# First attention: reciprocals of the sums in the loop, spread by a ones product; keys over twelve steps and weighing in each next step

## What is computed

```python
q = (query @ Wq).reshape(b, sq, NUM_HEADS, HEAD_DIM).transpose(0, 2, 1, 3)   # query = layernorm(x): 16 x 64 x 512
k = (key @ Wk).reshape(b, sk, NUM_KV_HEADS, HEAD_DIM).transpose(0, 2, 1, 3)  # key = value = ctx_4096: 16 x 1601 x 512
v = (value @ Wv).reshape(b, sk, NUM_KV_HEADS, HEAD_DIM).transpose(0, 2, 1, 3)
k, v = jnp.repeat(k, rep, axis=1), jnp.repeat(v, rep, axis=1)                # 32 heads on 8 key heads, HEAD_DIM 16
scores = jnp.einsum('bhqd,bhkd->bhqk', q, k) * scale
out = jnp.einsum('bhqk,bhkd->bhqd', jax.nn.softmax(scores, axis=-1), v)
x = x + out.transpose(0, 2, 1, 3).reshape(b, sq, DIM) @ Wo
```

## Time and profile before

| | us |
|---|---|
| median of 3 runs | 4194.62 (4188.19 to 4211.88) |
| the profiled execution | 4190.97, of which 4189.2 are the span from first to last instruction |
| the loop, first scores to last copy of OT | 117 to 1036 |
| `project_out`, first DMA to last addition | 1039 to 1115 |
| the rest (first scan, first feed-forward, second layer) | 1116 to 4189 |

### The profile page before, as it was taken

One profiled execution on the slowest core, in us unless ns is written; L12 is line 12 of the kernel. 1 busy time (PEld: TensorE's weight loads), 2 busy tenths in 40 slices (PEclk: granted clock), 3 DMA queues, 4 the chain that ended last, 5 costly groups with the idle time before them and its releaser, 6 DMA issues. The chain is left out here.

```text
span 4189.2 us, 72516 instructions
## 1 busy us (share of the span) xinstructions
PE 3589.1 (86%) x31360; PEld 2387.9 (57%) x31360; DVE 2325.6 (56%) x2671; ACT 1356.0 (32%) x1764; POOL 1396.8 (33%) x892
## 2 busy tenths in 40 slices
PE   6899999997556469999999999999999989565677
PEld 3566666664222245777777878777778645222224
DVE  3566566663299772444444444444444234798972
ACT  1455555554154010222222222222222111444430
POOL 4344444440089110111111111111111001596971
PEclk8899999998789779999999999999999998687999
DMA  6455555541422032111111111111111210221211
GB/s 183 125 138 138 151 139 141 144 122 44 69 68 73 27 118 77 32 44 37 45 38 45 38 45 38 46 38 43 41 40 40 89 58 3 79 81 55 81 48 38
DMA packets 216517, 303.62 MB, mean 72 GB/s; under 512 B 64856, under 2 KB 161688, under 8 KB 214792
## 3 DMA queue, kind: packets, MB, share of 16 engines
q1 hardware_dynamic: 216200, 299.00, 24.6%
HBM read 245.38 MB, written 53.10 MB: 71 GB/s over the span
## 5 line engine op out<-in xcount | busy, mean ns | idle before, releaser
L1336 POOL TENSOR_TENSOR D_ctx_lo<-D_ctx_raw,D_ctx_hi 128x1904 fp32r<-128x1904 f32 x64 | 255.0, 3985 | 1291.0 <-ACT D_ctx_hi L1330 1291.0
L580 DVE TENSOR_REDUCE A_mxc<-A_psX 128x2 f32<-128x768 f32 (+2 forms) x512 | 489.3, 990 | 255.9 <-PE A_psX L610 253.6
L800 ACT ACTIVATE A_probs<-A_psE 128x1024 f32<-128x1024 f32 (+1 forms) x416 | 426.5, 1025 | 316.6 <-PE A_psE L824 310.6
L1354 ACT ACTIVATE D_V<-D_psY 119x384 f32<-119x384 f32 x224 | 110.0, 491 | 842.5 <-PE D_psY L1421 842.5
L1370 DVE TENSOR_REDUCE D_mxc<-D_psE 128x4 f32<-128x1904 f32 (+1 forms) x128 | 242.3, 1893 | 190.6 <-PE D_psE L1440 190.3
L1652 ACT ACTIVATE D_probs<-D_psE 119x2048 f32<-119x2048 f32 x112 | 210.6, 1880 | 420.0 <-PE D_psE L1779 420.0
L234 POOL TENSOR_TENSOR ES_dBx<-E_du,E_Bn 128x512 f32<-128x512 f32 x256 | 317.0, 1270 | 70.7 <-POOLq L49 69.0
L1421 PE MATMUL D_psY<-D_wv_hi,D_ctx_hi 128*119 128x384 f32 (+1 forms) x896 | 314.6, 351 | 16.5 <-DVE D_K_lo L1365 9.0
L1697 DVE TENSOR_TENSOR D_acc<-D_acc,D_probs 119x1024 f32<-119x1024 f32 x96 | 117.7, 1226 | 354.3 <-ACT D_probs L1652 354.3
L1793 PE MATMUL D_psO<-D_probs,D_V 119*32 119x256 f32 (+1 forms) x5376 | 313.3, 381 | 0.0
L1421 PE MATMUL D_psY<-D_wv_hi,D_ctx_lo 128*119 128x384 f32 (+1 forms) x896 | 302.1, 337 | 0.0
(11 more groups left out here) (310 smaller groups left out, 7364.9 us busy)
## 6 DMA issues: line engine op xcount, KB each, us to landing
D_ctx_raw<-in_ctx SPq DMA_DIRECT2D x48, 952.0 KB, 5.2
A_land<-in_ctx SPq DMA_DIRECT2D x32, 768.0 KB, 5.0
A_land<-in_ctx SPq DMA_DIRECT2D x16, 1024.0 KB, 5.5
E_Bn<-bc_scratch SPq DMA_DIRECT2D x64, 256.0 KB, 3.6
E_Cn<-bc_scratch SPq DMA_DIRECT2D x64, 256.0 KB, 3.4
k_scratch<-A_Khl SPq DMA_DIRECT2D x32, 384.0 KB, 5.6
A_Kst<-k_scratch SPq DMA_DIRECT2D x64, 192.0 KB, 3.5
A_land<-in_ctx SPq DMA_DIRECT2D x16, 642.0 KB, 4.4
```

The costliest lines, as they stand in the source:

```text
L580: nc.vector.tensor_reduce(mxc[:, u % 4, :, u // 4], psX[:, x % 2, :, 0:w], axis=AX_X, op=ALU.max).then_inc(x_free, 1)
L800: nc.scalar.activation(probs[0:KW[k], n % NPR, :, :].rearrange("p h q -> p (h q)"), psE[0:KW[k], :], ACT.Exp, scale=HD ** -0.5).then_inc(e ...
L1336: nc.gpsimd.tensor_tensor(ctx_lo[c][:, :, 0:w], ctx_raw[c][:, :, 0:w], ctx_hi[c][:, :, 0:w].bitcast(F32), ALU.subtract).then_inc(lo_done[c ...
```

## The change

There are three parts, all in the first attention.

1. **Reciprocals in the loop.** DVE takes the reciprocal of the whole OT tile of a period (RT, 128 x 256) two periods later: between units 3 and 4 of `read_maxima(s)` it inverts period s - 2. SP saves the four rows of reciprocals to den_scratch, one DMA a period, issued behind the save of the next period's OT. psO is cleared to 1.0 instead of 0.0, so that unused rows have a reciprocal.
2. **`project_out` rewritten.** SP loads the reciprocals as 8 rows (rec), oT in quarters of 256 tokens (8 DMAs of 64 KB each), and wo behind the first quarter. POOL makes sel, which has ones where a row belongs to a head. PE multiplies sel by rec into psR, which spreads each reciprocal over its head's 16 rows. DVE multiplies oT by psR tile by tile. PE now goes tile by tile, four products for one of eight token tiles, with four banks for the results, and spreads tile t + 2 behind tile t. The additions to X follow two tiles behind.
3. **Order in the loop.** K_STEPS gives each chunk of keys three steps (twelve in all, four passes each; before 3, 2, 3, 2 with 4 or 6 passes). Weigh of step n - 1 stands in each step n. Before, it was two weighs in each odd step (one at step 1 of a batch and one at its step 0).

```diff
@@ project_out
             @block.sync
             def _(sp):
...
+                sp.dma_start(rec[:, :, :], rec_scratch).then_inc(rec_in, 16)
+                for n in range(TOK // QT):
+                    for half in range(2):
+                        src = o_scratch[half].rearrange("(h r) g t -> h r g t", r=32)[:, 0:hd, :, bass.ts(n, QT)]
+                        for h in range(heads // 2):
+                            row = half_rows * half + hd * h
+                            sp.dma_start(oT[row:row + hd, :, bass.ts(n, QT)], src[h]).then_inc(o_in[n], 16)
+                    if n == 0:
                         sp.dma_start(wo[:, :, :], Wo).then_inc(w_in, 16)
-                if x_scratch is not None:
-                    sp.dma_start(X[:, :, :], x_scratch).then_inc(x_in, 16)
+
+            @block.gpsimd
+            def _(pool):
+                nc.gpsimd.tensor_copy(sel[:, :, :], consts["ident"][0:heads, 0:heads].unsqueeze(2)
+                                      .broadcast_to([heads, heads, hd])).then_inc(sel_made, 1)
 
             @block.vector
             def _(dve):
-                dve.wait_ge(den_in, 16 * heads)
-                nc.vector.reciprocal(den[:, :], den[:, :]).then_inc(recip, 1)
-                for m in range(M):
-                    dve.wait_ge(chunk_in[m], 16 * len(o_rows[m]) + 16 * len(pieces(m)))
-                    for g in range(G):
-                        nc.vector.tensor_tensor(oT[:, m, g, :], oT[:, m, g, :], R[:, m, g, :],
-                                                ALU.mult).then_inc(scaled, 1)
-                if x_scratch is not None:
-                    dve.wait_ge(x_in, 16)
+                def add(t):
+                    dve.wait_ge(full, t + 1)
+                    nc.vector.tensor_tensor(X[:, t, :], ps[:, t % 4, :], X[:, t, :], ALU.add).then_inc(added, 1)
+
                 for t in range(NPAIR):
-                    dve.wait_ge(full, t + 1)
-                    nc.vector.tensor_tensor(X[:, t, :], ps[:, t, :], X[:, t, :], ALU.add)
+                    dve.wait_ge(o_in[t * P // QT], 16 * heads)
+                    dve.wait_ge(spread, t + 1)
+                    nc.vector.tensor_tensor(on[:, :, bass.ts(t, P)], oT[:, :, bass.ts(t, P)],
+                                            psR[:, t % 2, :].rearrange("p (g t) -> p g t", g=G), ALU.mult
+                                            ).then_inc(normed, 1)
+                    if t >= 2:
+                        add(t - 2)
+                for t in range(NPAIR - 2, NPAIR):
+                    add(t)
 
             @block.tensor
             def _(pe):
+                def spread_out(t):
+                    if t >= 2:
+                        pe.wait_ge(normed, t - 1)
+                    nc.tensor.matmul(psR[:, t % 2, :], sel[:, :, :].rearrange("k h d -> k (h d)"),
+                                     rec[:, :, bass.ts(t, P)], start=True, stop=True).then_inc(spread, 1)
+
+                pe.wait_ge(sel_made, 1)
+                pe.wait_ge(rec_in, 16)
+                spread_out(0)
+                spread_out(1)
                 pe.wait_ge(w_in, 16)
-                for n in range(M * G):
-                    pe.wait_ge(scaled, n + 1)
-                    for t in range(NPAIR):
-                        last = nc.tensor.matmul(ps[:, t, :], oT[:, n // G, n % G, bass.ts(t, P)], wo[:, n % G * M + n // G, :],
-                                                start=(n == 0), stop=(n == M * G - 1), skip_group_check=True)
-                        if n == M * G - 1:
-                            last.then_inc(full, 1)
+                for t in range(NPAIR):
+                    pe.wait_ge(normed, t + 1)
+                    if t >= 4:
+                        pe.wait_ge(added, t - 3)
+                    for g in range(G):
+                        last = nc.tensor.matmul(ps[:, t % 4, :], on[:, g, bass.ts(t, P)], wo[:, g, :],
+                                                start=(g == 0), stop=(g == G - 1))
+                    last.then_inc(full, 1)
+                    if t + 2 < NPAIR:
+                        spread_out(t + 2)
...
@@ l0_attention
-    K_STEPS = [(0, 3), (3, 2), (5, 3), (8, 2)]
+    K_STEPS = [(0, 3), (3, 3), (6, 3), (9, 3)]
...
+            def read_maxima(dve, link, b, g, between=None):
                 for u in range(NU):
+                    if between and u == 4:
+                        between()
...
+                            if s:
+                                save_reciprocals(s - 1)
+
+                        def save_reciprocals(s):
+                            sp.wait_ge(inverted, s + 1)
+                            sp.dma_start(den_scratch[HG * (s % 2):HG * (s % 2) + HG, :, bass.ts(s // 2, S)],
+                                         RT[HD:P:32, s % 2, :].rearrange("p (g t) -> p g t", t=S)
+                                         ).then_inc(rec_out[s % 2], 16)
 
                         sp.wait_ge(made, 1)
                         rows_of_ones(sp, 1)
                             for c in range(NC - 1):
                                 reload(sp, NC * j + c)
                         save(2 * B - 1)
+                        save_reciprocals(2 * B - 1)
                         for p in range(2):
                             sp.wait_ge(o_out[p], 16 * B)
+                            sp.wait_ge(rec_out[p], 16 * B)
...
+                                act.wait_ge(inverted, s - 1)
...
+                        def invert(s):
+                            dve.wait_ge(o_copied, s + 1)
+                            if s >= 2:
+                                dve.wait_ge(rec_out[s % 2], 16 * (s // 2))
+                            nc.vector.reciprocal(RT[:, s % 2, :], OT[:, s % 2, :]).then_inc(inverted, 1)
+
+                        nc.vector.memset(psO[:, 0:HQ], 1.0).then_inc(sums_cleared, 1)
                         for s in range(1, 2 * B):
-                            read_maxima(dve, link, s // 2, s % 2)
+                            read_maxima(dve, link, s // 2, s % 2, (lambda: invert(s - 2)) if s >= 2 else None)
+                        for s in range(2 * B - 2, 2 * B):
+                            invert(s)
...
-                            if n and n % STEPS == 0:
-                                weigh(n - 1)
-                            elif n % 2:
-                                if n % STEPS > 1:
-                                    weigh(n - 2)
+                            if n:
                                 weigh(n - 1)
...
+        RT = r.sb("RT", [P, 2, HQ])
```

More of the change, by code:

```diff
@@ L311, in scan_states, with project_out @@
         r.restart()
[L314 removed]
+def project_out(nc, consts, tag, X, o_scratch, rec_scratch, Wo, heads, hd):
     G = 4
[L317 removed]
+    QT = 256
     with ExitStack() as stack:
         r = Region(nc, stack, tag)
[L320 to L339 removed]
+        wo = r.sb("wo", [P, G, D])
+        oT = r.sb("oT", [P, G, TOK])
+        on = r.sb("on", [P, G, TOK])
+        rec = r.sb("rec", [heads, G, TOK])
+        sel = r.sb("sel", [heads, heads, hd])
+        ps = r.ps("ps", [P, 4, 512])
+        psR = r.ps("psR", [P, 2, 512])
+        w_in, rec_in, sel_made = r.sem("w_in"), r.sem("rec_in"), r.sem("sel_made")
+        o_in = [r.sem(f"o_in{n}") for n in range(TOK // QT)]
+        spread, normed, full, added = r.sem("spread"), r.sem("normed"), r.sem("full"), r.sem("added")
+        half_rows = heads * hd // 2
         with nc.Block() as block:
@@ L469, in l0_attention @@
         o_out = [r.sem(f"o_out{b}") for b in range(2)]
+        inverted = r.sem("inverted")
+        rec_out = [r.sem(f"rec_out{b}") for b in range(2)]
         k_rows = k_scratch.rearrange("j (d p o) n -> o (j d) p n", p=NPH, o=2)
@@ L910, in l0_attention @@
         step_body(False)
[L912 to L914 removed]
+    project_out(nc, consts, "A2", X, o_scratch, den_scratch, Wo.rearrange("(g p) n -> p g n", p=P), H, HD)
 def softplus(nc, act, a_sem, base, z, spare):
```

42 lines of the change are left out of this document (removed).

## The result

| us | before | after |
|---|---|---|
| median of 4 runs each | 4197.99 (4188.19 to 4211.88) | 4156.29 (4154.86 to 4156.87) |
| the profiled execution | 4190.97, span 4189.2 | 4156.77, span 4155.0 |
| first scores of the loop | 117.07 | 115.89 |
| a batch, mean of the 13 other than 0 and 12 | 57.34 | 57.17 |
| last copy of OT starts | 1035.65 | 1026.24 |

The ratio of the times is 0.9898, with a 95% interval of 0.9868 to 0.9927: about 1% faster.

A forecast was written before the change was run, and what follows sets the result against it. PE sets the loop's pace, with a serial tail behind it. Terms -30.5 + 1.9 + 0 + 5.4 + 0.7 - 3.3 = -25.8 us from 4190.97 gave 4165 us, range 4150 to 4184.

The forecast's parts named there:

- Output projection: Serial tail after the loop: from first DMA to last addition 45.7 us instead of 76.2, so -30.5 us.
- T0 + 10: Output projection: PE's main products start 10 us after its first DMA, when wo lands; ends 9.0 and 14.3.
- End of the loop: After the last OT copy: the last reciprocal delays the output projection's first DMA, +1.9 us with semaphores.
- Weighing and key order: Loop batches: idle time only exchanged for group changes; -0.16 us a batch, -2.4 over 15, booked as 0.
- the term of +0.86 for step 12: Step 12 of each period: holds 1.25 us of work, so still idles 0.43, twice a batch.
- Reciprocals: Maxima reads in the loop: PE waits for DVE, 0.36 us a batch, +5.4 over 15 batches (0 to 12.9).
- The brackets announced at unit 7: Sign in the loop: new PE idle brackets at unit 7 of the maxima, released by DVE, 0.05 to 0.4 us.
- The last but one period: No projection there: unit 6 waits for DVE, +1, less 0.3 for the pairs, so +0.7 us.
- The last period: At the lower clock, one weigh a step fits under the exponential; five step pairs and last weigh earlier: -3.3 us.
- (1): Rival: reciprocals hold PE up more, 12.9 instead of 5.4, with singles at 0.58: 4180 us; chance 0.18.
- (2): Rival: transfers set the output projection's start, 14.3 us after its first DMA: 4169 to 4171 us; chance 0.08.
- (3): Rival: loop gains the -2.4, DVE waits are hidden, last period keeps full clock: about 4154 us; chance 0.10.

The follow-up runs named there:

- e8: e4 with oT loaded in whole 16-KB rows (eight DMAs of 256 KB) instead of quarters: 4158.43 us, ratio 0.9929.
- e7: e6 with four banks for psR and the spread products in pairs behind every second tile: 4148.61 us, ratio 0.9905.
- e11: e4 with the spreads of four tiles ahead of the main products, the other four in pairs behind tiles 1 and 3: 4144.72 us, ratio 0.9879.
- e1: The kernel before with only the new order in the loop (key steps and single weighs): 4173.0 us, ratio 0.9952.
- e3: The kernel after with the new order of keys and weighs undone: 4183.0 us, ratio 0.9977.
- e4: The kernel after with DVE's reciprocal behind the last read of the maxima instead of between units 3 and 4: 4147.39 us, ratio 0.9891.
- e10: The kernel after, unchanged, timed once more in the third group: 4158.43 us, ratio 0.9917.
- e2: The kernel before with the new key steps alone, weighs still in pairs: 4179.66 us, ratio 0.9974.
- e9: The kernel before with the keys in eight steps, so that steps 8 to 12 idle: 4199.92 us, ratio 1.0021.
- e6: e4 with wo issued from ACT's queue at the start of the output projection: 4147.98 us, ratio 0.9906.

## Why the prediction was right or wrong

**Output projection: -26.1, forecast -30.5.** The mechanism is as told, and the start was met (T0 + 11.24, forecast T0 + 10, announced 9 to 15), though not for the reason given for T0 + 10: that the 1-KB pieces are faster than the 16-KB rows bought nothing, since the first quarter came at 105 GB/s, paced by its issues, against 114 (e8). The timeline of the kernel after, from the first DMA to the last addition:

```profile
1030.99 0.30 SPq L337 DMA_DIRECT2D A_rec<-den_scratch  x1
1031.34 5.05 SPq L343 DMA_DIRECT2D A_oT<-o_scratch  x8
1035.53 3.75 PE L374 MATMUL A_psR<-A_rec,A_sel 8*128 8x512 f32 x4 [9.36 <-DMA A_rec<-den_scratch]
1036.43 0.59 SPq L345 DMA_DIRECT2D A_wo<-in_L_xattn_Wo  x1
...
1042.23 6.64 PE L387 MATMUL A_ps<-A_wo,A_on 128*128 128x512 f32 x8 [2.95 <-DMA A_wo<-in_L_xattn_Wo]
1048.80 1.12 PE L374 MATMUL A_psR<-A_rec,A_sel 8*128 8x512 f32 x2
1049.85 3.70 PE L387 MATMUL A_ps<-A_wo,A_on 128*128 128x512 f32 x8
...
1053.48 1.12 PE L374 MATMUL A_psR<-A_rec,A_sel 8*128 8x512 f32 x2
...
1077.00 0.69 DVE L356 TENSOR_TENSOR all_X<-A_ps,all_X 128x512 f32<-128x512 f32 x1 [2.27 <-PE A_ps L387]
1080.43 0.69 DVE L356 TENSOR_TENSOR all_X<-A_ps,all_X 128x512 f32<-128x512 f32 x1 [2.74 <-PE A_ps L387]
```

Two terms were mis-sized. Ahead of PE: an issue with a three-dimensional pattern took 5.05 / 8 = 0.63 us and not the 3.57 / 8 = 0.45 of the plain rows, so wo was issued at T0 + 5.4, and it landed 5.8 later: +1.2. (In e8, with plain rows, eight issues take 3.55 again.) On PE: from the first main product to the end it took 1081.12 - 1042.23 = 38.9 where 35.7 were booked. The pitch of a tile is 1053.48 - 1048.80 = 4.68: 1.05 for the spread, where the forecast took the 0.86 of a main product, and 3.63 for four main products, 0.91 each. A tile without a change ahead of it takes 1080.43 - 1077.00 = 3.43, and the first, which began at the lower clock, took 1048.80 - 1042.23 = 6.57, so 3.1 more. The 29.64 of before held 29.64 - 32 x 0.86 = 2.1 of that kind, which leaves 1.0. The rest, 6 x (4.68 - 4.30) = 2.3 for the six spreads between the products, is the change between products of different shape, some 0.2 us each and two a spread. Together that is 3.3, against the 3.2 by which the booking was missed. A price of this kind had been seen for weigh, and was booked there and not here. e7 and e11 bear it out: in pairs a spread costs 0.955. The Trainium skill, TensorEngine Tiling (Array Packing), section Key Properties, states the drain at a change of the tiling mode; the spreads have 8 rows and the products 128. Whether that is a change of mode no trace here says; the runs give the price, 0.2 us a change.

The page DMA: Bandwidth & Descriptors of the Trainium skill, section Bandwidth, which wants batches of 1 MiB, was weighed against the cut into quarters. On the rate the trace agrees with it, 377 GB/s for the 1 MB of wo against 105 for pieces of 64 KB. What decides here is what has to land first, and the measurement decides for the quarters by 11 us (e8).

**End of the loop: +1.2, forecast +1.9.** Right within its size; the OT DMA overlaps with part of it.

**Weighing and key order: booked 0, measured -8.4 in 13 batches.** This is the step that failed. The -8.4 are e1's -0.65 in each of the 13 batches other than 0 and 12; the reciprocals then take most of it back, to the -2.2 seen. The forecast had the right parts (less idle, dearer singles) and came to -0.16 a batch; e1 measured -0.65. The price of the singles held: +1.6 a batch, 0.56 each. What failed is the term of +0.86 for step 12, which was to idle 0.43 twice a batch. The timeline of PE in e1, step 12 of a first period up to the next scores:

```profile
599.53 0.45 PE L824 MATMUL A_psE<-A_Qst,A_Kst 50*65 50x256 f32 x4
599.91 0.63 PE L839 MATMUL A_psO<-A_probs,A_V 128*17 128x256 f32 x8
600.47 0.50 PE L610 MATMUL A_psX<-A_Kst,A_Qst 50*128 50x512 f32 x2
601.18 0.51 PE L824 MATMUL A_psE<-A_Qst,A_Kst 50*128 50x256 f32 x4 [0.21 <-ACT A_probs L800]
```

The same step in the kernel before, behind its scores at 607.20:

```profile
607.49 0.40 PE L610 MATMUL A_psX<-A_Kst,A_Qst 50*128 50x512 f32 x2
608.85 0.50 PE L824 MATMUL A_psE<-A_Qst,A_Kst 50*128 50x256 f32 x4 [0.96 <-ACT A_probs L800]
```

The step lasts 1.65, near the 1.68 that the forecast took for its floor. But it holds 0.38 of scores, 0.56 of weigh and 0.50 for the maxima unit, 1.44 in all, where the forecast had 1.25 with a unit at 0.34. The unit stands behind weigh there, at 0.50; before, it followed the scores directly, at 0.40. Idle is 0.21, twice a batch, so the term is +0.42: +1.65 - 2.67 + 0.42 = -0.60, and -0.65 was measured. PE's work rose by 1.6 in all, no more than the split weighs cost, so the dearer unit of step 12 must be made up for elsewhere in the batch; where, the runs don't show. That the -0.16 was then booked as 0 put another 2.4 us beside it.

**Reciprocals: 0.47 a batch, forecast 0.36 (0 to 0.86).** Right in place and size. e3 against before and after against e4 both give 0.47. Fifteen batches: 7.1 us instead of 5.4. The brackets announced at unit 7, the second unit of step 4, aren't in PE's rows; the wait shows in the starts. In a second period of the kernel after the unit comes 0.48 behind its scores (the two rows below), in e4 0.24; in a first period of the kernel after 0.30.

```profile
669.48 0.40 PE L849 MATMUL A_psE<-A_Qst,A_Kst 50*128 50x256 f32 x4
669.96 0.44 PE L615 MATMUL A_psX<-A_Kst,A_Qst 50*128 50x384 f32 x2
```

**The last but one period: +3.0, forecast +0.7.** The wait was told (+1), not the fall of the clock behind it. The timeline of the kernel after there:

```profile
981.96 0.45 PE L615 MATMUL A_psX<-A_Kst,A_Qst 50*128 50x384 f32 x2 [1.26 <-DVE A_mxc L585]
...
985.15 1.05 PE L864 MATMUL A_psO<-A_probs,A_V 128*17 128x256 f32 x8
```

After 1.26 us of idle, weigh lasts 1.05 instead of 0.63 from about 983 us on: the clock fell a period earlier than before. In e4 that wait doesn't exist, and the stretch stays at the full level (970 to 991 us, clock in the last but two columns):

```profile
970.00:991.00 21.00, 18.09 (x188) 8.15 (x188) 17.32 (x21) 12.76 (x14) 0.00 (x0) 1.00 0.03 7
```

The period takes 21.8 us in e4 and e1 and 25.15 in the kernel after. In e10 the clock fell there again, behind a wait of 1.27, and the period took 26.9. The two profiles of the kernel after, with the wait, show the fall, and so does e3 (993.8), which has the same place for the reciprocal; e1, e2, e4 to e8 and e11, without it, don't. It isn't the only thing that brings it: e9, which has no reciprocals in the loop, fell at 995.9 as well. e3 and e9 fell behind a wait of 0.7 for the exponential, so the wait for DVE goes with the fall here but isn't shown to be its cause.

**The last period: -2.7 and -0.5, forecast -3.3.** Right, by the mechanism told. All steps are equal, 1.98 us from scores to scores (1001.54, 1003.52, 1005.49), with 0.19 of idle ahead of each.

**The sum.** Measured less forecast: output projection +4.4, end of the loop -0.7, 13 batches -2.2 - 4.7 = -6.9, batches 0 and 12 -5.9 - 0.7 = -6.6, last but one period +2.3, last +0.1, before the loop -1.2. Together -8.6, against the 8.4 by which the profiled gain was missed. Misses of both signs cancel in it: without the start and the two batches with a fall, +6.8 stands against -7.6, and that the total came within 9 us is in part luck.

**What had no term.** About -5.9 in batches 0 and 12 lie where the clock stood lower in before, and -1.2 ahead of the loop, in code that didn't change: the loop starts at 115.7 to 117.1 us over all profiles, so that is scatter. The forecast had no term for them. In one execution they could as well have been absent; whether the new order keeps the falls away on the whole is open, as said above. The median gained 41.7 and the profiled execution 34.2 because the four runs of before scatter upward (4188 to 4212; in e10 it is 31.5). Of the signs announced, batches of 57.3 to 57.7 and a part of 45 to 50 us were just missed (57.17, 50.1). Of the rivals, (1) was right that reciprocals cost more than counted, by 1.7 us and not 7.5; (2) saw that the transfers set the start, which e6 supports, but not at T0 + 14.3; (3) came nearest to the total (4154). Its first reason was right, the loop gains from the order, and by more than the 2.4 booked; the other two were wrong: the waits for DVE are not hidden and the last period is at the lower clock.

## What to carry to other kernels

When work is spread over steps that are bound by a chain, price each group that stays in a thin step by a row of that same step, since a short group alone between two others costs more than its share of a long one, and book the difference that comes out instead of calling it even. An extra operation on an engine that only has slack on the mean belongs behind the last of its double-buffered readers: here the place alone was worth some 7 us in the loop and 3 in a tail where the clock fell behind the wait. In a serial tail, cut what can follow and put it behind what the first product needs: here the order gave the gain, not a better rate; and give each switch between products of different shape its own price.

## What the runs showed of the hardware that was not expected

- A DMA issue took 0.45 us for plain rows and 0.63 us for pieces with a third dimension, from the same queue.
- The granted clock fell to its lower level for 3 to 10 us inside a loop in which PE is over 95% busy. All five falls seen came 0.5 to 1.7 us behind an idle time of about 1 us, but most such idle times had no fall behind them. The cause is open.
- Issuing wo at T0 from ACT's queue and not behind nine issues of SP's (e6) put the first product at T0 + 11.1; from its place in SP's queue it came at T0 + 11.2, 11.5 and 12.6. In e6 the DMA engines were busy 0.98 from 3 us behind T0 on.
- oT came at 114 GB/s in rows of 16 KB, with the DMA engines busy 0.95, and at 105 in pieces of 1 KB, with the engines busy 0.59; wo moved at 377.
- A change between products of 8 and of 128 rows cost some 0.2 us (a tile of 3.63 us between single spreads, two in 7.06 us between pairs).
